# Softmax sums of a cross-attention moved from VectorE to ScalarE, and the work between its units laid out anew

## The chip, the cores and the metric

One core of one Trainium2 chip runs the whole kernel as one program. The metric is the device time of an execution in microseconds, here the median of several runs. The engines are TensorE (PE, matrix products), VectorE (DVE), ScalarE (ACT), GpSimd (POOL) and SyncE (SP, which issues the DMAs); each runs its own list of instructions in order, and semaphores tie the lists together.

## The reference, cut to what matters

The reference is a decoder of two layers on x of 2 x 1024 x 256, all float32, with a layer norm after each part: a quaternion self-attention, a two-hop memory attention on a context of 2 x 77 x 256, eight experts, then in the second layer a long convolution, a cross-attention on the same context, and a quantised gated FFN. The change lies where the convolution part ends and the cross-attention runs:

```python
# convolution part (_L1_attn_ref): K = C * sigmoid(A)**t * B, causal
out = conv(x, K) + D * x
x = _layernorm(x + _layer_norm(x + gelu(out) @ W_proj.T + b_proj, gamma, beta))
# cross-attention (_L1_xattn_ref): 16 heads of 16, keys and values from ctx_1024 (77 rows)
attn = softmax(einsum('bhqd,bhkd->bhqk', q, k) / sqrt(16), axis=-1)
out = einsum('bhqk,bhkd->bhqd', attn, v)
out = out.transpose(0, 2, 1, 3).reshape(B, -1, D) @ Wo.T + bo
x = _layernorm(x + out)
```

## The kernel before, in words

The 2048 rows of x are 16 tiles of 128 rows, in four groups of four. The cross-attention goes through `UX` = 32 units: unit n is tile n // 2 and half n % 2 of the heads (8 heads, `HC`), so a group is 8 units (g = n // 8, m = n % 8). It starts while the last expert and the end of the convolution part (its group 3 of rows, and its norms for groups 2 and 3) are still to be done; these are interleaved with the first 17 units. All orders are written out by hand, one loop over the units for each engine.

A unit goes through these steps. TensorE: `xa_scores(n)` (line 2048) writes the scores of 8 heads x 77 columns into two PSUM banks; two pairs of banks take turns, so scores(n) wait for the exponentials of unit n - 2. VectorE: `lowest(n)` (line 1402) reduces them to one minimum for each head (the scores are computed negated). ScalarE: `numer(n)` (line 777) makes 8 exponentials of 128 x 77 with that minimum as bias. VectorE: `denom(n)` sums them over the 77 columns (line 1409) and takes the reciprocal (line 1410). POOL: `weights(n)` (line 528) multiplies. TensorE: `p_turn(n)` (lines 2062 to 2065) transposes the weights. ScalarE: `p_evac(n)` (lines 787, 788) copies them to SBUF.

In ScalarE's and TensorE's loop, unit n's transposes stand with the scores and exponentials of unit n + 3 (`AHEAD` = 3). TensorE's turn of the loop is scores(n + 3), at m = 4 `queries` of the next group (line 2033), p_turn(n), then what is due there: `xa_values` (lines 2082, 2084) of the group before at m = 0 and 1, `xa_out` (line 2095) at m = 5 and 6, `x_turn4` (line 2026, the next group's rows transposed) at m = 2 (m = 3 for group 0), and at n = 6 `projected(3)` (line 1992), the projection of conv group 3. ScalarE's turn is p_evac(n), copies of transposes (`xT_evac`, line 676), at n = 5 the two gelus of conv group 3 (`conv_gelu`, line 740, another table set, so a table load before and one after), then numer(n + 3). `o_evac` (line 796) copies the values at m = 1 and 2, `q_evac` (line 769) the queries at m = 4. projected(3) waits for both gelus.

VectorE's turn is lowest(n + 3), denom(n + 2), then an entry of the table `between` (line 1457): `convolved(3, k, part)`, part 0 a multiply (line 1309) and a scan (1310), part 1 two more (1314, 1315); `conv_out` (1336), `conv_stats` (1049, 1052), `conv_affine` in two parts of four instructions (1358, 1360), `x_stats` and `x_norm` (1057) for the layer norms, `residual` (1417). POOL's turn is weights(n + 2), then the powers of the norms by the table `XA_LN` (line 74, lines 397 and 399), `x_plus_bproj(3)` at n = 1 (line 515), `x_plus_beta(3)` at n = 5 (line 518) and `x_plus_bo` (line 523) at n = 4, 12 and 20. Behind the 32 units follows the FFN.

Of the kernel before, what the change touches and what calls it, by code (L numbers as in the profile page):

```python
# [13 lines left out]
ALU = mybir.AluOpType  # L14
# [3 lines left out]
P = 128  # L18
# [46 lines left out]
AHEAD = 3  # L65
HP = HC // 2
# [7 lines left out]
XA_LN = {8: (LN_DN[5],), 11: (LN_DN[6],), 14: (LN_DN[7],), 17: (LN_E,), 23: (LN_E + 1,), 30: (LN_E + 2,)}  # L74
# [17 lines left out]
def decoder(nc, a, out):  # L92
    w_kept = nc.dram_tensor("w_kept", (P, 18, D), F32, kind="Internal").ap()
    with ExitStack() as ctx:
# [283 lines left out]
        def _(pool):  # L378
# [175 lines left out]
            for n in range(UX):  # L554
# [4 lines left out]
                if n == 1:  # L559
                    x_plus_bproj(3)  # L560
                if n == 5:
                    x_plus_beta(3)
                for step in XA_LN.get(n, ()):
                    ln_power(step, 4)
                if n % 8 == 4 and n // 8 + 1 < G4:
                    x_plus_bo(n // 8 + 1)
# [16 lines left out]
        def _(act):  # L583
# [187 lines left out]
            def numer(n):  # L771

                act.wait_ge(sem("xa_mn"), n + 1)
                if n >= 4:
                    act.wait_ge(sem("xa_ptr"), n - 3)
                for h in range(HC):
                    ins = act.activation(Ex[n % 4][:, h, :], PS[:, 2 * (n % 2) + h // 4, LC * (h % 4):LC * (h % 4) + LC], ACT.Exp,  # L777
                                         scale=-1.0, bias=mxs[:, 8 * (n % 4) + h:8 * (n % 4) + h + 1])
                ins.then_inc(sem("xa_e"), 1)
# [27 lines left out]
            for n in range(UX):  # L807
# [3 lines left out]
                if m in (1, 2) and g >= 1:  # L811
                    o_evac(g - 1, m - 1)
# [5 lines left out]
                if n == 3:  # L818
                    xT_evac(XA_N[1], 1, 6)
                if n == 5:  # L820
# [5 lines left out]
                if m == 2 and 1 <= g < G4 - 1:  # L826
# [65 lines left out]
        def _(dve):  # L892
# [407 lines left out]
            def convolved(g, k, part):  # L1300
# [4 lines left out]
                if part == 0:  # L1305
                    dve.wait_ge(sem("xgT"), CONV_N[g] + 1)
                    if g or k:
                        dve.wait_ge(sem("conv"), KD * g + k)
                    link(dve.tensor_tensor(conv_z, xt, Apow[:, k, at:at + 4 * P], ALU.mult))
                    link(dve.tensor_tensor_scan(r, ones.to_broadcast([P, 4 * P]), conv_z, carry[:, k:k + 1] if g % 2 else 0.0, ALU.mult, ALU.add))  # L1310
# [37 lines left out]
            def conv_affine(g, part):  # L1348
# [6 lines left out]
                for j in range(4):  # L1355
# [50 lines left out]
            def denom(n):  # L1406
                dve.wait_ge(sem("xa_e"), n + 1)
                sums = mxs[:, 32 + 8 * (n % 4):40 + 8 * (n % 4)]
                link(dve.tensor_reduce(sums, Ex[n % 4], AX.X, ALU.add))
# [47 lines left out]
            between = {2: lambda: (convolved(3, 0, 0), convolved(3, 0, 1)), 3: lambda: convolved(3, 1, 0), 4: lambda: convolved(3, 1, 1),  # L1457
# [789 lines left out]
```

## Time and profile before

| | us |
|---|---|
| median of 3 runs | 787.16 (781.5 to 787.8) |
| the profiled execution | 784.69 |
| its span, first to last instruction | 783.0 |
| TensorE busy in the span | 713.0 (91%) |
| ScalarE busy | 552.9 (71%) |
| VectorE busy | 505.3 (65%) |
| POOL busy | 194.4 (25%) |

The profile is of one execution. Its starts are microseconds from the start of the span. The cross-attention's units lie between about 480 and 617 us. Busy shares are over the whole span, whose stages differ, so they do not say what limits this one. A line such as "x8" merges instructions of one line that follow each other. The granted clock is TensorE's, 1.00 being its full 2.4 GHz.

### The profile page before, as it was taken

The numbers are of one execution on the slowest core, as the hardware profiler recorded it, in microseconds if no ns is written. First come the engines' busy times: TensorE is split into PE (matmuls) and PEld (weight loads), VectorE is DVE, ScalarE is ACT, GpSimd is POOL, SyncE is SP. The second block draws the span as 40 slices with busy tenths as digits, with TensorE's granted clock in tenths as the row PEclk, the third lists the DMA queues.
The fourth block names the chain that finished last, engine by engine and source line by source line (L and its number), as shares of the span: only waits on it lengthen the run. The fifth ranks groups of instructions, "written<-read, shape, count | busy, mean of one in ns | idle before, by whom it ended". The sixth has DMA issues, their size and how long they took to land.

```text
span 783.0 us, 10853 instructions
## 1 busy us (share of the span) xinstructions
PE 713.0 (91%) x3850; PEld 387.3 (49%) x3850; DVE 505.3 (65%) x1181; ACT 552.9 (71%) x977; POOL 194.4 (25%) x246
## 2 busy tenths in 40 slices
PE   4999999989999999999999999889899999992797
PEld 2652222212222225888888886544455644440686
DVE  4794645753413224588647557979877687988776
ACT  3759999999999995464043345587687533898992
POOL 1661142201010000104253242465444100000022
PEclk9999999999999999999999999989899999996799
DMA  7412112141255160303326000010100000000002
GB/s 197 134 32 49 28 28 71 25 95 28 46 142 177 29 182 0 109 2 108 114 101 216 1 1 0 1 70 11 41 1 0 1 1 0 1 0 0 0 28 81
DMA packets 57389, 42.13 MB, mean 54 GB/s; under 512 B 36882, under 2 KB 54136, under 8 KB 57208
## 3 DMA queue, kind: packets, MB, share of 16 engines
q1 hardware_dynamic: 57192, 41.31, 19.1%
q8 instruction: 31, 0.51, 0.3%
q14 instruction: 22, 0.18, 0.1%
q10 hardware_dynamic: 144, 0.13, 0.1%
HBM read 28.59 MB, written 4.46 MB: 42 GB/s over the span
## 4 chain that ended last, share of the span: by engine, by line
PE 56%; ACT 22%; DVE 15%; issue 3%; DMA 1%; SPq 1%; POOL 1%; POOLq 0%; ACTq 0%; DVEq 0%
ACT arena L654 12%; PE banks L1658 8%; PE banks L2207 7%; PE banks L1962 7%; PE banks L1978 6%; PE banks L1644 4%; PE banks L1628 2%; PE banks L1992 2%; ACT arena L878 2%; DVE arena L1486 2%; DVE arena L1049 2%; ACT arena L879 2%; PE banks L1818 2%; ACT arena L867 1%; PE banks L2095 1%
## 5 line engine op out<-in xcount | busy, mean ns | idle before, releaser
L654 ACT ACTIVATE arena<-banks 128x1024 f32<-128x1024 f32 x256 | 239.7, 1047 | 6.5 <-PE banks L1658 4.1
L1658 PE MATMUL banks<-arena 128*32 128x512 f32 x1024 | 136.4, 604 | 2.6 <-DVE arena L1125 2.4
L1644 PE MATMUL banks<-arena 64*128 64x512 f16 x512 | 86.4, 383 | 10.1 <-ACT arena L654 5.8
L2207 PE MATMUL banks<-arena 128*128 128x512 f32 x192 | 83.1, 594 | 1.1 <-DVE arena L1502 0.9
L397 POOL TENSOR_SCALAR arena<-arena 128x2 f32<-128x2 f32 (+2 forms) x39 | 11.8, 302 | 256.2 <-DVE arena L1052 256.2
L1644 PEld LDWEIGHTS banks<-arena 64*128 64x128 f16 x512 | 20.9, 93 | 108.7 <-ACT arena L654 98.9
L777 ACT ACTIVATE arena<-banks,arena 128x77 f32<-128x77 f32 x256 | 59.3, 369 | 19.5 <-DVE arena L1402 19.5
L735 ACT ACTIVATE arena<-banks,arena 128x256 f32<-128x256 f32 x64 | 26.9, 471 | 49.3 <-PE banks L1962 49.3
L2207 PEld LDWEIGHTS banks<-arena 128*128 128x128 f32 x192 | 36.2, 190 | 47.4 <-issue 43.4
L1978 PE MATMUL banks<-arena 128*128 128x256 f32 x256 | 56.5, 380 | 1.2 <-ACT arena L676 1.2
L1962 PE MATMUL banks<-arena 128*128 128x256 f32 x256 | 56.2, 379 | 0.0
L528 POOL TENSOR_TENSOR arena<-arena 128x616 f32<-128x616 f32 x32 | 40.7, 1271 | 56.4 <-DVE arena L1410 56.4
L1978 PEld LDWEIGHTS banks<-arena 128*128 128x128 f32 x256 | 48.2, 190 | 8.6 <-issue 2.2
L1962 PEld LDWEIGHTS banks<-arena 128*128 128x128 f32 x256 | 48.5, 190 | 6.5
L846 ACT ACTIVATE arena<-banks 128x512 f32<-128x512 f32 x48 | 28.1, 609 | 30.4 <-PE banks L2207 30.4
L1057 DVE TENSOR_SCALAR arena<-arena 128x256 f32<-128x256 f32 x96 | 37.4, 442 | 18.1 <-POOL arena L399 18.1
L1125 DVE COPY arena<-banks 128x512 f32<-128x512 f32 x16 | 10.9, 683 | 51.3 <-PE banks L1658 51.3
L2219 PE MATMUL banks<-arena 128*128 128x256 f32 x192 | 41.7, 380 | 0.8 <-ACT arena L886 0.8
L1658 PEld LDWEIGHTS banks<-arena 128*32 128x32 f32 x1024 | 20.4, 107 | 42.7 <-issue 42.7
L1049 DVE BATCH_NORM_STATS2 arena<-arena 128x6 f32<-128x256 f32 x112 | 40.2, 413 | 1.1
L2219 PEld LDWEIGHTS banks<-arena 128*128 128x128 f32 x192 | 36.4, 190 | 6.2 <-ACT arena L886 1.2
L399 POOL TENSOR_TENSOR arena<-arena 128x2 f32<-128x2 f32 (+2 forms) x39 | 36.9, 946 | 3.3
(263 smaller groups left out, 1258.4 us busy)
## 6 DMA issues: line engine op xcount, KB each, us to landing
arena<-in_L_ffn_w SPq DMA_DIRECT2D x16, 1024.0 KB, 7.4
w_kept<-arena SPq DMA_DIRECT2D x3, 768.0 KB, 3.6
arena<-w_kept SPq DMA_DIRECT2D x3, 768.0 KB, 4.7
arena<-in_x SPq DMA_DIRECT2D x4, 512.0 KB, 7.9
out_x<-arena SPq DMA_DIRECT2D x3, 512.0 KB, 2.9
arena<-in_L_ffn_b SPq DMA_DIRECT2D x1, 1024.0 KB, 9.2
arena<-in_L_ffn_w_gate SPq DMA_DIRECT2D x1, 768.0 KB, 7.8
arena<-in_L_ffn_w_up SPq DMA_DIRECT2D x1, 768.0 KB, 9.5
```

The source lines that it names most:

```text
L399: pool.tensor_tensor(rstd[:, at:at + n], veps[:, at:at + n], expo[:, at:at + n], ALU.pow).then_inc(sem("ln_rstd"), 1)
L528: pool.tensor_tensor(Ex[n % 4], Ex[n % 4], rdx[:, n % 4, :, None].to_broadcast([P, HC, LC]), ALU.mult).then_inc(sem("xa_w"), 1)
L654: act.activation(PT[kt % 2][:, half], PS[:, 2 * (n % 3):2 * (n % 3) + 2, :], ACT.Exp, scale=DH ** -0.5 / QK_UP ** 2).then_inc(sem("exp_don ...
L777: ins = act.activation(Ex[n % 4][:, h, :], PS[:, 2 * (n % 2) + h // 4, LC * (h % 4):LC * (h % 4) + LC], ACT.Exp, scale=-1.0, bias=mxs[:, 8 ...
L1049: ins = dve.bn_stats(bstat[:, at + j, :], view(j))
L1057: ins = dve.tensor_scalar(dst(j), src(j), mv[:, at + j, 0:1], rstd[:, at + j:at + j + 1], ALU.subtract, ALU.mult)
L1644: mm = pe.matmul(bank(2 * (n % 3) + h), KT[u % 2][64 * h:64 * h + 64, P * kt:P * kt + P], QT[u % 2][64 * h:64 * h + 64, 512 * half:512 * h ...
L1658: mm = pe.matmul(PS[32 * j:32 * j + 32, 6, :], VS[w][:, kt, h, :], PT[kt % 2][:, half, h, :], start=(kt == 0), stop=(kt == TB - 1))
L1962: mm = pe.matmul(PS[:, f // 2, 256 * (f % 2):256 * (f % 2) + 256], W1r[r][:, k, P * f:P * f + P], XT[:, k, TE * P * e:TE * P * e + TE * P] ...
L1978: mm = pe.matmul(bank(Y_BANK[e])[:, D * j:D * j + D], hT[e % 2][:, f, P * j:P * j + P], W2r[r][:, f, :], start=(f == 0), stop=(f == FT - 1))
L2207: mm = pe.matmul(bank(2 + n % 4), (wgT if n < IC * G4 else wuT)[:, k, P * c:P * c + P], XT[:, k, 512 * g:512 * g + 512], start=(k == 0), s ...
L2219: mm = pe.matmul(o, UF[:, c, P * t:P * t + P], wdT[:, c, :], start=(c == 0), stop=(c == IC - 1))
```

## The change

In units 2 to 17 (`OWN_SUMS`) each of the 8 exponentials writes its own sum (`accum_out`), and `denom` there keeps the reciprocal alone. The sums are of the same values. The entries between the units are laid out anew on all engines: the pieces of conv group 3 are spread over more of VectorE's turns, `conv_gelu(3, k)` goes from ScalarE's turn 5 to 7, `projected(3)` from TensorE's turn 6 to 7, values and their copies of group 0 one turn later, x_turn4(2) one turn later, x_plus_bproj(3), x_plus_beta(3) and x_plus_bo to later turns of POOL.

```diff
--- before.py
+++ after.py
@@ -63,6 +63,8 @@
 
 UX = T * KD
 AHEAD = 3
+OWN_SUMS = range(2, 18)
+VALUES_AT = (1, 0, 0)
 HP = HC // 2
 HEAD2 = P - LC
 SPLIT = LC - HEAD2
@@ -71,7 +73,9 @@
 V_BANK = (7, 6)
 VALUES_IN = {None: (6, slice(0, 512)), 0: (6, slice(0, 256)), 1: (2, slice(256, 512))}
 
-XA_LN = {8: (LN_DN[5],), 11: (LN_DN[6],), 14: (LN_DN[7],), 17: (LN_E,), 23: (LN_E + 1,), 30: (LN_E + 2,)}
+XA_LN = {6: (LN_DN[5],), 9: (LN_DN[6],), 15: (LN_DN[7],), 17: (LN_E,), 23: (LN_E + 1,), 30: (LN_E + 2,)}
+
+XA_BO = (17, 20, 25)
 
 RSQRT_SEED = 0x5F3759DF
 PROJ_BANK = ((6, 7), (6, 7), (5, 7), (6, 7))
@@ -556,14 +560,14 @@
                     weights(n + 2)
                 if n == 0:
                     ln_power(LN_CN[E - 1], 2, 4)
-                if n == 1:
-                    x_plus_bproj(3)
-                if n == 5:
-                    x_plus_beta(3)
                 for step in XA_LN.get(n, ()):
                     ln_power(step, 4)
-                if n % 8 == 4 and n // 8 + 1 < G4:
-                    x_plus_bo(n // 8 + 1)
+                if n == 6:
+                    x_plus_bproj(3)
+                if n == 8:
+                    x_plus_beta(3)
+                if n in XA_BO:
+                    x_plus_bo(1 + XA_BO.index(n))
             for half in range(2):
                 ln_power(LN_E + 3 + half, 2, 2 * half)
             def largest(n, col):
@@ -774,8 +778,10 @@
                 if n >= 4:
                     act.wait_ge(sem("xa_ptr"), n - 3)
                 for h in range(HC):
+                    at = 8 * (n % 4) + h
+                    own = {"accum_out": mxs[:, 32 + at:33 + at]} if n in OWN_SUMS else {}
                     ins = act.activation(Ex[n % 4][:, h, :], PS[:, 2 * (n % 2) + h // 4, LC * (h % 4):LC * (h % 4) + LC], ACT.Exp,
-                                         scale=-1.0, bias=mxs[:, 8 * (n % 4) + h:8 * (n % 4) + h + 1])
+                                         scale=-1.0, bias=mxs[:, at:at + 1], **own)
                 ins.then_inc(sem("xa_e"), 1)
 
             def p_evac(n):
@@ -808,22 +814,22 @@
                 g, m = n // 8, n % 8
                 for i in WQ_AT.get(n, ()):
                     wq_evac(i)
-                if m in (1, 2) and g >= 1:
-                    o_evac(g - 1, m - 1)
+                if g >= 1 and m - VALUES_AT[g - 1] in (1, 2):
+                    o_evac(g - 1, m - VALUES_AT[g - 1] - 1)
                 if m == 4 and g + 1 < G4:
                     q_evac(g + 1)
                 p_evac(n)
                 if n == 2:
                     xT_evac(CONV_N[3], 3, 6)
-                if n == 3:
-                    xT_evac(XA_N[1], 1, 6)
-                if n == 5:
+                if n in (3, 11):
+                    xT_evac(XA_N[g + 1], g + 1, 6)
+                if n == 7:
 
                     conv_gelu(3, 0)
                     conv_gelu(3, 1)
                 if n + AHEAD < UX:
                     numer(n + AHEAD)
-                if m == 2 and 1 <= g < G4 - 1:
+                if m == 2 and g == 2:
                     xT_evac(XA_N[g + 1], g + 1, 6)
                 if n in (UX - 3, UX - 2):
                     o_evac(G4 - 1, n - UX + 3, 0)
@@ -1297,17 +1303,19 @@
                     ins = dve.tensor_scalar(CBrev[:, k, :], Apow[:, k, ::-1], convC[:, k:k + 1], convB[:, k:k + 1], ALU.mult, ALU.mult)
                 link(ins)
 
-            def convolved(g, k, part):
+            def convolved(g, k, part, steps=(0, 1)):
 
                 at = 4 * P * (g % 2)
                 xt = XT[:, k, 4 * P * g:4 * P * g + 4 * P]
                 r = conv_r[g][k]
                 if part == 0:
-                    dve.wait_ge(sem("xgT"), CONV_N[g] + 1)
-                    if g or k:
-                        dve.wait_ge(sem("conv"), KD * g + k)
-                    link(dve.tensor_tensor(conv_z, xt, Apow[:, k, at:at + 4 * P], ALU.mult))
-                    link(dve.tensor_tensor_scan(r, ones.to_broadcast([P, 4 * P]), conv_z, carry[:, k:k + 1] if g % 2 else 0.0, ALU.mult, ALU.add))
+                    if 0 in steps:
+                        dve.wait_ge(sem("xgT"), CONV_N[g] + 1)
+                        if g or k:
+                            dve.wait_ge(sem("conv"), KD * g + k)
+                        link(dve.tensor_tensor(conv_z, xt, Apow[:, k, at:at + 4 * P], ALU.mult))
+                    if 1 in steps:
+                        link(dve.tensor_tensor_scan(r, ones.to_broadcast([P, 4 * P]), conv_z, carry[:, k:k + 1] if g % 2 else 0.0, ALU.mult, ALU.add))
                 else:
                     if g % 2 == 0:
                         dve.tensor_copy(carry[:, k:k + 1], r[:, 4 * P - 1:4 * P])
@@ -1345,14 +1353,14 @@
                 dve.wait_ge(sem("proj_y"), g + 1)
                 stats((lambda j: XB3[g][:, j, :], 4)).then_inc(sem("ln_stat"), 1)
 
-            def conv_affine(g, part):
+            def conv_affine(g, part, tiles=range(4)):
 
                 if part == 0:
                     dve.wait_ge(sem("ln_stat"), LN_DN[2 * g] + 1)
                 else:
                     dve.wait_ge(sem("ln_rstd"), LN_DN[2 * g] + 1)
                     dve.wait_ge(sem("x3_plus"), 2 * g + 2)
-                for j in range(4):
+                for j in tiles:
                     xb = XB3[g][:, j, :]
                     if part == 0:
                         ins = dve.scalar_tensor_tensor(xb, xb, mv[:, j, 0:1], bc1[:, 1, :], ALU.subtract, ALU.mult)
@@ -1406,7 +1414,8 @@
             def denom(n):
                 dve.wait_ge(sem("xa_e"), n + 1)
                 sums = mxs[:, 32 + 8 * (n % 4):40 + 8 * (n % 4)]
-                link(dve.tensor_reduce(sums, Ex[n % 4], AX.X, ALU.add))
+                if n not in OWN_SUMS:
+                    link(dve.tensor_reduce(sums, Ex[n % 4], AX.X, ALU.add))
                 dve.reciprocal(rdx[:, n % 4, :], sums).then_inc(sem("xa_rs"), 1)
 
             def residual(g, half):
@@ -1454,11 +1463,16 @@
             expert_norm(E - 1, 4)
             denom(3)
 
-            between = {2: lambda: (convolved(3, 0, 0), convolved(3, 0, 1)), 3: lambda: convolved(3, 1, 0), 4: lambda: convolved(3, 1, 1),
-                       7: lambda: (conv_out(3), x_stats(2)), 9: lambda: x_norm(LN_DN[5], 2).then_inc(sem("ln_d2"), 1),
-                       10: lambda: conv_stats(3), 11: lambda: conv_affine(3, 0), 12: lambda: conv_affine(3, 1), 13: lambda: x_stats(3),
-                       14: lambda: residual(0, 0), 16: lambda: x_norm(LN_DN[7], 3).then_inc(sem("ln_d2"), 1),
-                       15: lambda: residual(0, 1), 17: lambda: xa_stats(0), 18: lambda: xa_norm(0),
+            between = {2: lambda: convolved(3, 0, 0),
+                       3: lambda: (convolved(3, 0, 1), convolved(3, 1, 0, (0,))),
+                       4: lambda: convolved(3, 1, 0, (1,)), 5: lambda: convolved(3, 1, 1),
+                       6: lambda: x_stats(2), 7: lambda: x_norm(LN_DN[5], 2).then_inc(sem("ln_d2"), 1),
+                       8: lambda: conv_out(3), 9: lambda: conv_stats(3),
+                       10: lambda: conv_affine(3, 0, (0, 1)), 11: lambda: conv_affine(3, 0, (2, 3)),
+                       12: lambda: conv_affine(3, 1, (0, 1)), 13: lambda: conv_affine(3, 1, (2, 3)),
+                       14: lambda: residual(0, 0), 15: lambda: (residual(0, 1), x_stats(3)),
+                       16: lambda: x_norm(LN_DN[7], 3).then_inc(sem("ln_d2"), 1),
+                       17: lambda: xa_stats(0), 18: lambda: xa_norm(0),
                        22: lambda: residual(1, 0), 23: lambda: (residual(1, 1), xa_stats(1)), 24: lambda: xa_norm(1),
                        28: lambda: residual(2, 0), 29: lambda: residual(2, 1), 30: lambda: xa_stats(2), 31: lambda: xa_norm(2)}
             for n in range(2, UX):
@@ -2158,15 +2172,15 @@
                     x_group_turn("ln_c", E, CONV_N[3], 3, b0=6)
                 if g >= 1:
 
-                    if m < KD:
-                        xa_values(g - 1, m, range(NC5))
+                    if 0 <= m - VALUES_AT[g - 1] < KD:
+                        xa_values(g - 1, m - VALUES_AT[g - 1], range(NC5))
 
                     first = 5 if g < G4 - 1 else 3
                     if m in (first, first + 1):
                         xa_out(g - 1, m - first)
-                if m == (2 if g else 3) and g + 1 < G4:
+                if m == (2 if g == 2 else 3) and g + 1 < G4:
                     x_turn4(g + 1)
-                if n == 6:
+                if n == 7:
                     projected(3)
                 if n in (UX - 3, UX - 2):
                     xa_values(G4 - 1, n - UX + 3, range(NC5), 0)
```

## Rows read from the trace of the kernel before

**Rows 1.** Windows of 20 us: length, busy us by engine (instructions), PEclk, DMA.

```profile
490.00:510.00 20.00, 17.95 (x94) 10.73 (x92) 19.10 (x33) 10.79 (x38) 9.09 (x8) 1.00 0.01 1
510.00:530.00 20.00, 16.16 (x75) 9.07 (x75) 15.71 (x28) 17.01 (x57) 11.82 (x7) 0.83 0.22 79
```

**Rows 2.** Waits from 498 to 556 us: total us, times, longest.

```profile
ACT arena L777 <- DVE arena L1402: 11.3, 7, 4.0
...
ACT arena L787 <- PE banks L2065: 1.5, 3, 1.0
```

**Rows 3.** Timeline of ScalarE, memory attention: start us, us, engine line op.

```profile
331.04 0.31 ACT L689 ACTIVATE arena<-banks,arena 128x77 f32<-128x77 f32 x1
331.25 0.20 ACT L689 ACTIVATION_READ_ACCUMULATOR arena<-banks,arena 128x1 f32 x1
331.34 0.32 ACT L689 ACTIVATE arena<-banks,arena 128x77 f32<-128x77 f32 x1
```

**Rows 4.** Timeline of ScalarE, a unit's exponentials and what follows.

```profile
525.92 1.84 ACT L777 ACTIVATE arena<-banks,arena 128x77 f32<-128x77 f32 x8
527.59 0.67 ACT L787 ACTIVATE arena<-banks 128x512 f32<-128x512 f32 x1
```

**Rows 5.** Timeline of VectorE, one unit's denominator.

```profile
529.39 0.78 DVE L1409 TENSOR_REDUCE arena<-arena 128x8 f32<-128x616 f32 x1
530.21 0.20 DVE L1410 RECIPROCAL arena<-arena 128x8 f32<-128x8 f32 x1
```

**Rows 6.** Timeline of POOL and VectorE, conv group 3's two first multiplies.

```profile
501.97 2.35 POOL L515 TENSOR_TENSOR arena<-arena 128x1024 f32<-128x1024 f32 x1
...
502.25 2.62 DVE L1309 TENSOR_TENSOR arena<-arena 128x512 f32<-128x512 f32 x1
...
510.10 0.65 DVE L1309 TENSOR_TENSOR arena<-arena 128x512 f32<-128x512 f32 x1
```

**Rows 7.** Timeline of ScalarE around conv group 3's gelus [idle before].

```profile
509.28 1.84 ACT L777 ACTIVATE arena<-banks,arena 128x77 f32<-128x77 f32 x8 [3.98 <-DVE arena L1402]
...
515.93 0.34 ACT L788 ACTIVATE arena<-banks 128x128 f32<-128x128 f32 x1
516.29 1.28 ACT L740 ACT_TABLE_LOAD   x1
517.58 1.15 ACT L740 ACTIVATE arena<-arena 128x512 f32<-128x512 f32 x2
```

**Rows 8.** Timeline of TensorE, the two slow spells [idle before].

```profile
515.67 1.40 PE L2048 MATMUL banks<-arena 64*128 64x308 f32 x4 [1.28 <-ACT arena L777]
...
518.87 4.58 PE L1992 MATMUL banks<-arena 128*128 128x256 f32 x16
523.39 0.79 PE L2048 MATMUL banks<-arena 64*128 64x308 f32 x4
...
551.90 0.79 PE L2048 MATMUL banks<-arena 64*128 64x308 f32 x4 [0.73 <-ACT arena L777]
...
555.20 1.40 PE L2048 MATMUL banks<-arena 64*128 64x308 f32 x4 [1.46 <-ACT arena L777]
...
558.40 1.94 PE L2082 MATMUL banks<-arena 128*32 128x512 f32 x8
...
561.98 0.79 PE L2048 MATMUL banks<-arena 64*128 64x308 f32 x4
...
563.75 1.06 PE L2082 MATMUL banks<-arena 128*32 128x512 f32 x8
...
565.81 0.79 PE L2048 MATMUL banks<-arena 64*128 64x308 f32 x4
```

**Rows 9.** Windows of 2 us, columns as in rows 1.

```profile
516.00:518.00 2.00, 2.00 (x9) 1.04 (x7) 2.00 (x3) 1.97 (x4) 2.00 (x2) 0.50 0.00 0
556.00:558.00 2.00, 2.00 (x10) 1.09 (x7) 1.97 (x5) 1.53 (x8) 2.00 (x2) 0.50 0.03 8
```

**Rows 10.** Chain that ended last, an earlier group's projection: start us, us.

```profile
481.79 3.65 PE banks L1992 x16
```

## The prediction

> **What bounds the kernel now.** The order of reading was: windows over the stage of the cross-attention (about 480 to 620 us of the span), the waits inside 498 to 556 us, then the timelines of single engines there. The windows show no single bound: from 490 to 510 us VectorE is busy 19.10 of 20 us, TensorE 17.95 and ScalarE only 10.79; in the next 20 us ScalarE is at 17.01 and TensorE's granted clock averages 0.83 [rows 1]. So VectorE is full first, and the cure would seem to be what the change does. But the waits say how much of it can be had. Between 498 and 556 us ScalarE waits 11.3 us for VectorE's minima (line 1402, `lowest`), in 7 waits, and 1.5 us for TensorE's transposes [rows 2]. From 556 us on TensorE runs nearly without a gap until the stage ends, and its time there is the kernel's time. What counts, then, is when TensorE reaches that run.
>
> **The sums on ScalarE.** The trace has this very instruction in another stage: line 689 is an exponential of 128x77 from PSUM with a bias and a sum. Each is followed by a read of the accumulator of 0.20 us, but the pair starts 0.30 us after the pair before it [rows 3]. Without a sum eight take 1.84 us, and the next instruction starts 1.67 us after the first, so 0.21 us each [rows 4]. A unit of eight therefore costs ScalarE 8 x 0.30 = 2.40 instead of 1.67 us, 0.73 more, and its last sum is there 7 x 0.30 + 0.41 = 2.51 us after the first start instead of 1.84, 0.67 more. Over 16 units that is 11.7 us of ScalarE. The ends: nothing, if in a row of eight the reads hid behind the next exponential (the rows with sums stand in groups of at most six); 16 x 8 x 0.20 = 25.6 us, if each read were added whole. I take 11.7, since the pairs' own starts give it.
>
> **The sums off VectorE.** The reduce of line 1409 starts 0.82 us before the reciprocal [rows 5]. Sixteen go, 13.1 us of VectorE in all. On the way of one unit to its weights that is -0.82 + 0.67 = -0.15 us, so nothing: the gain can only be that VectorE comes earlier to the next `lowest`.
>
> **ScalarE's budget.** Of the 16 units, 4 to 17 lie between 498 and 556 us: 14 x 0.73 = 10.2 us more. These waits of ScalarE there are 11.3 + 1.5 = 12.8 us [rows 2]. Even if all of them went, numer(18) could be only 2.6 us earlier. The change takes 13.1 us from a full engine and puts 11.7 on one that has 12.8 us free, in pieces. This is the main term, and it is why I expect little.
>
> **The moved steps.** Before, the scan of conv group 3 was done in one piece behind unit 4's denominator, and its first multiply took 2.62 us beside a POOL addition of 2.35 us, where the next took 0.65 [rows 6]. That piece made numer(6) wait 3.98 us, until 509.28 [rows 7]. After the change POOL's x_plus_bproj(3) is gone from there and only multiply and scan (about 2.8 us) stand in it: lowest(6) can start about 504.7, but ScalarE has then numer(5) with sums and the copy of line 676 to do, so numer(6) starts near 505.8: 3.5 us earlier. The queries of group 1 then begin at 505.8, about as before, and scores(8) follow at 510.5. POOL's x_plus_bproj(3) and x_plus_beta(3) move behind units 6 and 8, where VectorE's x_norm may lose up to 2.4 us beside them; that lies under the stall below. The four affine halves no longer stand whole before a `lowest`. x_plus_bo (POOL, 2.4 us, three times) is needed only by the residuals of units 22, 28 and the end, and moves to 17, 20 and 25: nothing. SP's and POOL's DMA queues are passed by no step; the weights' loads wait for proj_mm, which comes before 530 either way, and are used after 603: nothing.
>
> **A new stall.** Before, the gelu of conv group 3 stood in ScalarE's unit 5 and `projected(3)` in TensorE's unit 6, so one unit lay between them. Now both stand in unit 7. TensorE's order is p_turn(7), projected(3); ScalarE's is p_evac(7), table load, two gelus. The copy cannot start before p_turn(7) ends, so TensorE must idle for 0.7 + 1.28 + 1.15 + 0.1 = 3.2 us (the copy, then load and gelus [rows 7], and the hand-overs). Queued behind it on TensorE are the scores of unit 11, on ScalarE numer(10). ScalarE comes to p_evac(7) only after numer(9), at about 519.8, since each numer before it is 0.73 longer; the gelus end at 522.85 and projected(3) runs from 522.9 to 526.6 at full clock. Before, it ran from 518.87 to 523.39 [rows 8], but had scores(10) and p_turn(7), 1.77 us, still behind it, so that scores(11) came at 525.2. They are 1.4 us later now.
>
> The Trainium skill (ScalarE: Activation LUTs, section What ACT_TABLE_LOAD costs) says that a switch to another table set costs a drain of about 1.38 us beside the load of 1.28. This trace shows the load 0.02 us after the end of the copy and the gelu right behind the load [rows 7], so no such drain there. By the page the stall would be 4.6 instead of 3.2 us, and the forecast 1.4 later.
>
> **From there to unit 17.** After projected(3), ScalarE's unit is 2.40 + 0.65 = 3.05 us and TensorE's 1.8 plus 2.05 for values, 1.0 for a turn, 1.9 for an output product, 3.6 for queries. Worked forward in order, each instruction starting when its engine and its inputs are free: scores(13) start at 532.4, scores(15) at 539.1, queries(2) at 540.25, scores(17) at 549.0, scores(18) at 552.7 and scores(19) at 554.5. Before, the last two were at 551.90 and 555.20 [rows 8]; the second ran at half clock.
>
> **The clock.** The granted clock falls to 0.50 of full (1.2 instead of 2.4 GHz) in two spells, around 516 to 520 and 555 to 561 us [rows 9], each after TensorE had idled. At full clock scores and p_turn take 563.75 - 561.98 = 1.77 us, projected(3)'s sixteen products 3.65 (the same line in an earlier group), values 565.81 - 563.75 = 2.06 [rows 8, 10]. Spell one: 518.87 - 515.67 = 3.20 for scores and turn, 4.52 for projected(3), so 1.43 + 0.87 = 2.3 us lost. Spell two: 3.20 again, and values 561.98 - 558.40 = 3.58, so 1.43 + 1.52 = 3.0 us [rows 8]. The idle before spell two was the 0.73 and 1.46 us ahead of scores(18) and (19) [rows 8]; the working above leaves about 0.3 us of it, so I take the spell as gone: values(1, 0) end at 558.7, where they ended at 561.98, 3.3 us earlier. Spell one stays: TensorE now idles 1.25, 1.15 and 4.2 us between 512 and 523. Some of it falls into the idle itself; I take that 3.7 us of work run at half clock, so 1.8 us lost, of which 0.5 us ScalarE's own pace would have taken anyway: 1.3 us.
>
> **Sum.** -3.3 + 1.3 = -2.0 us. The profiled execution took 784.69 us for a span of 783.0, so 782.7. It lies 2.5 us under the median of the three runs, 787.16 (781.5 to 787.8); against the median the same sum gives 785.2. I write 783.5, nearer the profiled one, since the sum is made on it. Behind 562 us nothing else changes: TensorE is without gaps, x_norm(3) ends near 560.7 as before, x_turn4(3) follows at 564.4, and the shift is carried to the end.
>
> **Rivals.** First, VectorE was the bound all along and the reads cost little: then TensorE's idle of 8.5 us between 498 and 556 and both spells (5.3 us) go, and only the stall of 3.2 stays (8.5 from summing the idle of TensorE's timeline in that stretch, of which rows 8 have the largest still standing, 1.28, 0.73 and 1.46): 784.7 - 8.5 - 5.3 + 3.2 = 774.1. For it: VectorE's 19.10 of 20 us. Against: the budget of ScalarE. Second, half way: sums at their 0.30, but the spell at projected(3) falls wholly into the idle, and the affine's relief is worth more than I give: -6, 778.7. Third, on the other side: TensorE, now waiting for a ScalarE at 3.05 us a unit, idles in pieces of half a microsecond in units 10 to 17, and a third spell of low clock comes on top, while spell two stays. It decides from the point where TensorE's idle in 545 to 556 us is again 2 us. Price: -3.3 becomes -0.3, +1.3 stays, and one spell more is +3.0: +4, 788.7. For it: 2.2 us of idle were enough for spell two. Against: the scores(18) no longer wait for the affine. Fourth, the change doesn't do what it says: the sums are written but the path through ScalarE takes all back, within 1 us of 784.7.
>
> **Chances.** Forecast (-5 to +1 on the profiled time) 0.45; fourth rival 0.20; second 0.13; first 0.08; third 0.14. About 1%, 7.9 us, is what a measurement of this kernel can tell from no change. Faster by over 1%: the first and a third of the second, 0.13; slower by over 1%: 0.05, the third with the upper ends of the reads' cost; within: 0.82. The range 777.5 to 789 leaves out the first rival and the far end of the reads' cost.
>
> **What would show it.** Right: pairs of line 777 at 0.30 us in units 2 to 17, 11 to 12 us more of ScalarE busy, 16 reduces fewer; numer(6) near 505.8; TensorE idle of 3.2 to 4.3 us before line 1992 with a clock of 0.5 near it; no spell near 556. Wrong: reads that add nothing or 0.2 us each; a wait before line 1992 under 2 us; a spell of low clock in units 10 to 17; a gain over 8 us.

## The result, and the profile after

The changed kernel took 790.94 us (median of 12 runs, 789.74 to 793.53) beside 785.64 us for the kernel before (12 runs): ratio 1.0066, 95% interval 1.0049 to 1.0083. It is slower by 5.3 us (5.2 by the ratio) where 2 us less were forecast, and outside the range. Its profiled execution took 791.63 us for a span of 789.9. Four executions of the kernels below (849 us with the gelus in turn 6; 927, 1190 and 1411 us with both edits) were slow ones and count in no ratio.

Section 1 of its page:

```profile
PE 714.6 (90%) x3850; PEld 388.4 (49%) x3850; DVE 494.4 (63%) x1165; ACT 563.9 (71%) x1105; POOL 194.1 (25%) x246
```

The sums went where the change says: VectorE has 16 instructions and 10.9 us less, ScalarE 128 more and 11.0 us more. ScalarE's figure is near the prediction's 11.7. The 16 reduces that went had taken 12.6 us, for 13.1 forecast; VectorE's total fell by less because two norms take 2.0 us longer each, which the shorter steps of conv group 3 make good only in part. The next view is the one of [rows 1], windows of 20 us:

```profile
490.00:510.00 20.00, 17.46 (x97) 11.92 (x96) 17.16 (x39) 15.59 (x81) 9.12 (x9) 1.00 0.00 1
510.00:530.00 20.00, 12.88 (x55) 7.57 (x54) 14.01 (x25) 18.96 (x89) 9.63 (x7) 0.85 0.00 0
...
570.00:590.00 20.00, 17.35 (x80) 10.38 (x79) 14.86 (x26) 13.70 (x51) 11.68 (x10) 0.91 0.04 17
```

VectorE is no longer full (17.16 of 20 us for 19.10), ScalarE is (18.96 between 510 and 530), and TensorE is busy only 12.88 us there, where it was 16.16. A stretch with a lowered clock has appeared at 570 to 590, where the kernel before has none.

The span of this execution is 6.9 us longer than that of before, but not all of it belongs to the change. The projection of conv group 2, ahead of the first changed unit, starts at 485.04 here and at 481.72 before. So starts have to be compared from a common point. I take the start of the sixteen products of the last expert's second tile (491.37 before, 494.69 after) and follow the stage to the first of the transposes behind it that waits (619.27 before, 626.24 after): 127.90 and 131.55 us. The stage costs 3.65 us more. TensorE's waits in it add up to 16.0 us, before to 11.1. TensorE's timeline shows where, as [rows 8] did:

```profile
520.29 0.79 PE L2062 MATMUL banks<-arena 64*128 64x308 f32 x4 [1.26 <-ACT arena L783]
...
526.51 5.83 PE L2006 MATMUL banks<-arena 128*128 128x256 f32 x16 [4.37 <-ACT arena L744]
532.27 0.79 PE L2062 MATMUL banks<-arena 64*128 64x308 f32 x4
...
561.01 0.79 PE L2062 MATMUL banks<-arena 64*128 64x308 f32 x4
...
564.97 0.79 PE L2062 MATMUL banks<-arena 64*128 64x308 f32 x4
...
581.40 0.84 PE L2062 MATMUL banks<-arena 64*128 64x308 f32 x4 [2.65 <-ACT arena L773]
...
584.04 2.66 PE L2109 MATMUL banks<-arena 128*128 128x256 f32 x8
586.63 0.79 PE L2062 MATMUL banks<-arena 64*128 64x308 f32 x4
```

From the common point (the lines of this kernel are numbered some 14 higher): the projection (line 2006 here) starts 4.3 us later than before. Unit 11's scores, at 532.27, are 3.8 us late (37.58 against 525.17 - 491.37 = 33.80). Then the kernel catches up: unit 20's scores at 564.97 are at 70.28, before at 70.61 [rows 8]. The spell of low clock near 556 is gone, as forecast. But unit 24's scores (581.40, before 575.69) are 2.4 us late after a wait of 2.65, and unit 25's (586.63, before 579.66) 3.65 us, because the transposes behind unit 24's scores and the output product at 584.04 ran mostly at low clock. From there nothing changes. So there are two places: one, at 522 to 532, is made good again by 565; the other, at 578 to 586, is not.

The granted clock (last but two of the columns, as in [rows 9]) falls to 0.50, the 1.2 GHz level, at both, each time after TensorE has stood idle:

```profile
524.00:526.00 2.00, 0.00 (x0) 0.00 (x0) 2.00 (x2) 1.97 (x3) 2.00 (x2) 0.50 0.00 0
526.00:528.00 2.00, 1.49 (x4) 1.22 (x5) 1.91 (x4) 1.97 (x4) 1.11 (x1) 0.50 0.00 0
528.00:530.00 2.00, 2.00 (x6) 1.65 (x5) 0.00 (x0) 2.00 (x15) 0.00 (x0) 0.50 0.00 0
...
582.00:584.00 2.00, 2.00 (x9) 1.16 (x7) 1.05 (x2) 1.72 (x8) 2.00 (x2) 0.50 0.00 0
```

What made TensorE wait at 578 is in the timelines of VectorE and POOL. First POOL, then VectorE:

```profile
571.99 2.36 POOL L527 TENSOR_TENSOR arena<-arena 128x1024 f32<-128x1024 f32 x1
```

```profile
572.12 4.25 DVE L1063 TENSOR_SCALAR arena<-arena 128x256 f32<-128x256 f32 x4
576.40 1.22 DVE L1447 TENSOR_REDUCE arena<-arena 128x4 f32<-128x1024 f32 x1
577.53 0.79 DVE L1410 TENSOR_REDUCE arena<-banks 128x8 f32<-128x616 f32 x1
```

```profile
578.36 1.83 ACT L783 ACTIVATE arena<-banks,arena 128x77 f32<-128x77 f32 x8 [3.62 <-DVE arena L1410]
580.03 1.32 ACT L773 ACTIVATE arena<-banks,arena 128x512 f32<-128x512 f32 x2
```

The last two are ScalarE's. Line 527 is x_plus_bo(1), which the change moved from POOL's turn 4 to 17. It begins 0.13 us before VectorE's norm of group 0 (line 1063), whose four instructions took 2.23 us in the kernel before and now take 4.25. Behind the norm on VectorE stands lowest(22), behind that on ScalarE numer(22), which waits 3.62 us, and behind that the copies of the queries of group 3 (line 773), for which unit 24's scores wait.

### The profile page after: what moved, and what is told of

The parts are those of the page before. It is cut to its first block, busy times and chain, and to the rows that moved or that the text cites. A ratio compares the mean times of both kernels' runs of the same rounds, so it can differ in the third digit from the quotient of the medians.

```text
span 789.9 us, 10966 instructions
## 1 busy us (share of the span) xinstructions
PE 714.6 (90%) x3850; PEld 388.4 (49%) x3850; DVE 494.4 (63%) x1165; ACT 563.9 (71%) x1105; POOL 194.1 (25%) x246
## 4 chain that ended last, share of the span: by engine, by line
PE 54%; ACT 29%; DVE 12%; issue 3%; SPq 1%; DMA 1%; POOL 0%; POOLq 0%; ACTq 0%; DVEq 0%
ACT arena L658 14%; PE banks L1672 8%; PE banks L2221 7%; PE banks L1976 7%; PE banks L1992 6%; ACT arena L783 4%; PE banks L1658 4%; PE banks L1642 3%; PE banks L2006 2%; ACT arena L884 2%; DVE arena L1500 2%; ACT arena L885 2%; PE banks L1832 2%; DVE arena L1063 2%; PE banks L2109 2%
## 5 line engine op out<-in xcount | busy, mean ns | idle before, releaser
L783 ACT ACTIVATE arena<-banks,arena 128x77 f32<-128x77 f32 x256 | 70.0, 390 | 11.6 <-DVE arena L1410 11.4
L1063 DVE TENSOR_SCALAR arena<-arena 128x256 f32<-128x256 f32 x96 | 41.4, 483 | 17.4 <-POOL arena L403 17.4
L1131 DVE COPY arena<-banks 128x512 f32<-128x512 f32 x16 | 10.9, 683 | 52.3 <-PE banks L1672 52.3
```

The source lines that it names most:

```text
L1063: ins = dve.tensor_scalar(dst(j), src(j), mv[:, at + j, 0:1], rstd[:, at + j:at + j + 1], ALU.subtract, ALU.mult)
```

## The experiments

The theories at the outset: A, the order of two steps costs the time (the projection that waits for its own turn's gelus; x_plus_bo(1) beside the norm), and the sums cost next to nothing; B, the sums on ScalarE are the cost. "Stage" is the length defined above, from one profile each. "Clock lost" is worked out from windows of 2 us between 486 and 636 us of the same profile, the sum of (1 - granted clock) x 2 us; low clock in which TensorE stood idle is in it, so it is the most that the clock can have cost. Ratios are to the kernel before. The runs in one table, in the order of the text below:

| kernel | ratio (interval) | stage, us | clock lost, us |
|---|---|---|---|
| before | 1 | 127.90 | 6.8 |
| changed | 1.0066 (1.0049 to 1.0083) | 131.55 | 5.1 |
| gelus in turn 6 | 0.9991 (0.9975 to 1.0007) | 126.09 | 0 |
| x_plus_bo in 19 and 21 | 1.0014 (0.9995 to 1.0032) | 128.15 | 3.4 |
| sums alone | 0.9945 (0.9927 to 0.9963) | 124.90 | 1.7 |
| layout alone | 1.0031 (1.0014 to 1.0048) | 130.88 | 5.1 |
| both edits | 0.9949 (0.9923 to 0.9974) | 124.08 | 3.4 |
| both edits, no sums | 0.9969 (0.9947 to 0.9991) | 123.45 | 0 |
| sums, gelus and projection in turn 7 | 1.0001 (0.9981 to 1.0021) | 129.90 | 5.1 |
| sums, x_plus_bo in 17, 20, 25 | 0.9995 (0.9973 to 1.0018) | 127.58 | 3.4 |
| changed, wait filled | 1.0086 (1.0052 to 1.0121) | 134.27 | 3.4 |
| both edits, sums from unit 8 | 0.9954 (0.9931 to 0.9977) | 124.82 | 1.7 |
| sums from unit 8 alone | 0.9971 (0.9949 to 0.9992) | 124.44 | 3.4 |

**Gelus one turn earlier.** In ScalarE's list of the changed kernel:

```diff
-                if n == 7:
+                if n == 6:
                     conv_gelu(3, 0)
                     conv_gelu(3, 1)
```

> The changed kernel with one edit: ScalarE's gelus of conv group 3 stand in its turn 6, TensorE's projection stays in turn 7, so one unit lies between them again. Theory A (the order of two steps costs the time: the projection that waits for its own turn's gelus, and x_plus_bo(1) beside the norm of group 0): TensorE's 4.4 us wait before the projection falls under 1.5 us and the projection runs at full clock in 3.7 instead of 5.8 us; the stage is 4 to 6 us shorter than in the changed kernel, the time at or 1 us under the kernel before. Theory B (the sums on ScalarE are the cost, whatever the order): the wait goes, but ScalarE then holds up each unit, and less than 1.5 us is won.

Measured: 0.9991, against 1.0066 of the changed kernel. For its profile the same kernel was run once more:

> The same kernel as the one with the gelus in turn 6, for its profile: the wait before the projection under 1.5 us, the projection 3.7 us long, and the wait before the scores of unit 24 (2.65 us in the changed kernel) still there.

TensorE's timeline of that run:

```profile
522.60 3.72 PE L2006 MATMUL banks<-arena 128*128 128x256 f32 x16 [1.26 <-ACT arena L744]
526.48 0.79 PE L2062 MATMUL banks<-arena 64*128 64x308 f32 x4 [0.15 <-ACT arena L783]
529.58 0.79 PE L2062 MATMUL banks<-arena 64*128 64x308 f32 x4 [1.26 <-ACT arena L783]
...
576.66 0.79 PE L2062 MATMUL banks<-arena 64*128 64x308 f32 x4 [2.66 <-ACT arena L773]
```

The wait of 4.37 us is 1.26, the projection runs at full clock, the second wait is untouched (2.66). The stage is 5.5 us shorter than in the changed kernel. As A said. But only 3.9 of the 5.5 us are there when unit 24's scores start (82.78 us from the common point, in the changed kernel 86.71). The rest is that no low clock follows the second wait in this profile, as it did in the changed kernel.

**x_plus_bo two turns later.**

```diff
-XA_BO = (17, 20, 25)
+XA_BO = (19, 21, 25)
```

> The changed kernel with one edit: POOL's x_plus_bo of groups 1 and 2 stand in turns 19 and 21 instead of 17 and 20, so that the first no longer runs beside VectorE's norm of group 0. Theory A: the norm's four instructions take 2.2 instead of 4.25 us, TensorE's 2.65 us wait before the scores of unit 24 goes with the low clock after it, 3 to 4.5 us are won against the changed kernel. Theory B: the norm is shorter, but the wait at unit 24 comes from lateness that the sums had made before, so under 1 us is won.

Measured: 1.0014, 0.5% under the changed kernel, about 4 us; the stage is 3.4 us shorter. VectorE and TensorE in this kernel:

```profile
570.66 2.23 DVE L1063 TENSOR_SCALAR arena<-arena 128x256 f32<-128x256 f32 x4
```

```profile
577.93 0.79 PE L2062 MATMUL banks<-arena 64*128 64x308 f32 x4 [0.65 <-ACT arena L773]
578.67 0.63 PE L2076 MATMUL banks<-arena 128*128 128x128 f32 x4
579.14 0.27 PE L2077 MATMUL banks<-arena 128*64 128x128 f32 x1
579.34 0.43 PE L2079 MATMUL banks<-arena 128*64 128x128 f32 x2
579.71 1.99 PE L2109 MATMUL banks<-arena 128*128 128x256 f32 x8
```

The norm is back at 2.23 us, the wait is 0.65 instead of 2.65, the output product 1.99 instead of 2.66. As A said.

**The sums alone.** The kernel before with `OWN_SUMS = range(2, 18)`, `accum_out` in `numer` and the condition in `denom`, nothing moved.

> The kernel before with the sums of units 2 to 17 on ScalarE and nothing moved. Theory A: within 1.5 us of the kernel before, since ScalarE's waits of 11.3 us take the 10.2 us; the low clock near 516 us stays or is a little longer. Theory B: 4 to 6 us slower than the kernel before, as the changed kernel is.

Measured: 0.9945, 782.31 us, so 4.3 us faster by the ratio. Both theories missed: A had the size under 1.5 us, B had the other sign. The stage is 3.0 us shorter. TensorE's timeline, at the two places of [rows 8] and at a third:

```profile
519.90 3.72 PE L1996 MATMUL banks<-arena 128*128 128x256 f32 x16 [1.27 <-ACT arena L741]
...
555.81 0.79 PE L2052 MATMUL banks<-arena 64*128 64x308 f32 x4 [0.43 <-ACT arena L780]
...
593.66 0.79 PE L2052 MATMUL banks<-arena 64*128 64x308 f32 x4 [1.09 <-ACT arena L780]
```

Its waits over the stage add up to what they were before, 11.1 us in both, but none is over 1.3 us. The kernel before had, besides the waits in [rows 8], this longest one ahead of its first spell:

```profile
512.33 0.79 PE L2048 MATMUL banks<-arena 64*128 64x308 f32 x4 [2.37 <-ACT arena L769]
```

Both spells of low clock of the kernel before are gone: the projection takes 3.72 instead of 4.58 us, unit 19's scores 0.79 instead of 1.40. (This profile has one short spell elsewhere, at 594 to 600, after the wait of 1.09 us; the kernel before has that wait and no spell.) So what the sums give here is not less idle but a better clock: 1.7 us lost instead of 6.8. This does not hang on the two profiles alone. The mean granted clock over the whole span was 0.979 to 0.984 in the six runs of this kernel and 0.970 to 0.979 in the 29 of the kernel before; the difference of the means, 0.006 of 785 us, comes to some 5 us, an estimate of the size of the whole gain. It does not say where in the span they lie.

**The layout alone.**

```diff
-OWN_SUMS = range(2, 18)
+OWN_SUMS = range(0)
```

> The changed kernel with all sums on VectorE as before, so the new layout alone. Theory A: as slow as the changed kernel or slower (5 to 7 us over the kernel before), with the wait before the projection at 3.2 us or more and the wait at unit 24 in place. Theory B: faster than the changed kernel by 4 us or more, at the kernel before or under it.

Measured: 1.0031, the stage 3.0 us longer than before. Slower with no sum on ScalarE, so B falls. A had asked for 5 to 7 us and 2.4 came. This is 0.35% less than the changed kernel's 1.0066, with intervals that do not overlap, so in this layout the sums may cost something; but the medians differ by only 1.3 us (789.60 and 790.94, taken beside 787.02 and 785.64 of the kernel before) and the stages by 0.7. How much of the slowdown is the sums' stays open. TensorE:

```profile
524.27 6.24 PE L2006 MATMUL banks<-arena 128*128 128x256 f32 x16 [5.09 <-ACT arena L744]
...
579.14 0.79 PE L2062 MATMUL banks<-arena 64*128 64x308 f32 x4 [2.70 <-ACT arena L773]
```

Both waits are there in full. The wait before the projection does not come from ScalarE being late; it comes from the order.

**Both edits together.**

> The changed kernel with both edits: gelus of conv group 3 in ScalarE's turn 6, x_plus_bo of groups 1 and 2 in turns 19 and 21. Each alone gave back 4 to 5 us of the changed kernel's 5.2. Theory A (two faults of order, which add): both are given back, the time is 2 to 4 us under the kernel before, as with the sums alone (ratio 0.9945). Rival A2 (the lateness that the second fault adds lay behind the first): the two do not add, and the time stays within 1 us of the kernel before.

Measured: 0.9949, the stage 3.8 us shorter than before. The edits gave 0.75 and 0.52% singly and give 1.17% together, so they nearly add, and A2 falls. The ratio rests on seven runs.

**Both edits, no sums on ScalarE.**

> As the kernel with both edits, but all sums on VectorE as before: what the sums are worth in a layout without the two faults. With the sums on ScalarE worth 0.55% in the order of before, theory A expects 3 to 5 us more here than with both edits and the sums on ScalarE; a rival, that the spread pieces of conv group 3 alone do what the sums do, expects the two within 1.5 us.

Measured: 0.9969. The intervals of this and the kernel with the sums overlap, and the stage has the other sign. But the profile is of the fastest of its twelve runs, 779.96 us at a mean granted clock of 0.985: three lie at 780 to 781 us and nine at 784 to 787, at 0.977 to 0.979. A's 3 to 5 us did not come: by the ratios this kernel is 1.6 us slower than the one with the sums, and the intervals allow nothing as well as 3 us. That the spread pieces of conv group 3 do in the new order what the sums do in the old one, as the rival said, fits this and is not shown.

**The first fault by itself.** On the kernel with the sums alone:

```diff
-                if n == 5:
+                if n == 7:
                     conv_gelu(3, 0)
                     conv_gelu(3, 1)
...
-                if n == 6:
+                if n == 7:
                     projected(3)
```

> The kernel before with the sums on ScalarE, and conv group 3's gelus and its projection both moved to turn 7, nothing else: the first fault by itself. Theory A: TensorE waits 3.2 to 4.5 us before the projection and runs it at half clock, and the time is 3 to 5 us over the kernel with the sums alone. Rival: the wait only takes the place of others around it, and under 1.5 us is lost.

Measured: 1.0001 against 0.9945, so 4.4 us. TensorE:

```profile
524.53 6.36 PE L1996 MATMUL banks<-arena 128*128 128x256 f32 x16 [4.37 <-ACT arena L741]
```

The same wait of 4.37 us and the slow projection, in an otherwise old order. As A said. The stage is 5.0 us longer, but 1.7 of that is one more spell, at 506 to 510, which stands ahead of the edit and so is not its own.

**The second fault by itself.** On the kernel with the sums alone, POOL's list:

```diff
-                if n % 8 == 4 and n // 8 + 1 < G4:
-                    x_plus_bo(n // 8 + 1)
+                if n in (17, 20, 25):
+                    x_plus_bo(1 + (17, 20, 25).index(n))
```

> The kernel before with the sums on ScalarE, and POOL's three x_plus_bo in turns 17, 20 and 25 as in the changed kernel, nothing else: the second fault by itself. Theory A: the norm of group 0 takes 4.25 instead of 2.2 us, TensorE waits 2 to 2.7 us before the scores of unit 24, and the time is 2 to 4 us over the kernel with the sums alone (ratio to the kernel before about 0.998 to 1.000). Rival: without the first fault there is slack, and the ratio stays at 0.9945 within 0.001.

Measured: 0.9995 against 0.9945, 3.9 us. TensorE:

```profile
547.84 0.63 PE L2066 MATMUL banks<-arena 128*128 128x128 f32 x4 [0.23 <-ACT arena L791]
576.24 0.79 PE L2052 MATMUL banks<-arena 64*128 64x308 f32 x4 [2.09 <-ACT arena L770]
```

The wait is there, and between these two rows lie 28.4 us, where the kernel with the sums alone has 26.6 (546.88 to 573.49). So the place and the sign are as A said, the profile shows 1.8 us of delay there and a spell behind it (576 to 582). The collision is there too, POOL's addition first and VectorE's norm of group 0 after it:

```profile
566.83 2.35 POOL L524 TENSOR_TENSOR arena<-arena 128x1024 f32<-128x1024 f32 x1
566.95 4.24 DVE L1060 TENSOR_SCALAR arena<-arena 128x256 f32<-128x256 f32 x4
```

Here too a spell ahead of the edit (508 to 512) makes the stages a poor measure.

**The wait filled.** In TensorE's turn 7 of the changed kernel:

```diff
                 if n == 7:
+                    pe.wait_ge(sem("xa_q"), 4)
+                    for _ in range(9):
+                        pe.matmul(bank(6), ident, WpT.rearrange("p k d -> p (k d)"), start=True, stop=True)
                     projected(3)
```

> The changed kernel with nine products of 512 columns of a weight tile into bank 6 just before the projection, 3.9 us of work without use in TensorE's wait of 4.4 us; their result is overwritten. If the idle is what lowers the clock, the wait stays as long but the projection runs in 3.7 instead of 5.8 us, and 1.5 to 2.5 us are won against the changed kernel. Rival: the low clock has another cause (the time since the last spell, or the work of the other engines), and the projection stays at 5 to 6 us with nothing won.

Measured: 1.0086, the stage 2.7 us longer than in the changed kernel. TensorE, then the windows at 523 and 529 us:

```profile
522.35 7.99 PE L2186 MATMUL banks<-arena 128*128 128x512 f32 x18
530.18 3.62 PE L2006 MATMUL banks<-arena 128*128 128x256 f32 x16
533.73 0.79 PE L2062 MATMUL banks<-arena 64*128 64x308 f32 x4
```

```profile
523.00:525.00 2.00, 2.00 (x6) 0.84 (x5) 1.43 (x3) 1.98 (x8) 2.00 (x2) 1.00 0.00 0
...
529.00:531.00 2.00, 2.00 (x8) 1.21 (x7) 0.00 (x0) 1.61 (x11) 0.00 (x0) 1.00 0.00 0
```

The nine products are 18 instructions in the trace, 7.8 us in all, twice what I had reckoned, so they outlasted the wait by 3.5 us and nothing was won; the ratio is higher than the changed kernel's 1.0066, but the intervals overlap. But the clock stayed at full 2.4 GHz at this place, and the projection took 3.62 instead of 5.83 us. ScalarE, VectorE and POOL were busy for the same time over the span as in the changed kernel (563.9, 494.6 and 194.1 us for 563.9, 494.4 and 194.1). The four kernels with a wait of 4.37 us or more at this place all ran the projection at low clock; the one without the idle did not. So the low clock there follows TensorE's idle. Whether a filling of the right length pays was not tried.

**Sums from unit 8 only**, with both edits, and on the kernel before (`OWN_SUMS = range(8, 18)`):

> The kernel with both edits, but sums on ScalarE only in units 8 to 17; units 2 to 7 sum on VectorE. With both edits the sums on ScalarE gave TensorE waits of 1.15, 0.78 and 1.26 us in units 5 to 8, without them it waited 2.51 us for VectorE's conv_out in unit 9. If both are costs of their own, this one has neither and is 1 to 3 us faster than with the sums in 2 to 17, ratio 0.991 to 0.994. Rival: the sums are worth nothing in this layout, and the ratio stays between 0.994 and 0.998.

Measured: 0.9954: no better than with the sums from unit 2, the rival holds. Against the profile with both edits, the wait before unit 7's scores is gone (1.15 us there) and that before unit 9's is 0.56 instead of 1.26, but unit 10's scores wait 1.29 us.

> The kernel before with the sums of units 8 to 17 on ScalarE and nothing moved. If the gain of the sums alone (0.55%) comes from the units where VectorE's affine steps stood before the minima and led to the low clock near 556 us, it is kept whole: ratio 0.993 to 0.996. Rival: it comes from units 2 to 7, where the scan held up unit 6, and then most of it is gone: 0.998 to 1.000.

Measured: 0.9971, between the two expectations. Its profile tells why: the spell near 556 us is gone, the one at the projection is not.

```profile
517.30 0.79 PE L2052 MATMUL banks<-arena 64*128 64x308 f32 x4 [2.38 <-ACT arena L770]
520.65 1.40 PE L2052 MATMUL banks<-arena 64*128 64x308 f32 x4 [1.50 <-ACT arena L780]
523.86 4.78 PE L1996 MATMUL banks<-arena 128*128 128x256 f32 x16
...
559.67 0.79 PE L2052 MATMUL banks<-arena 64*128 64x308 f32 x4 [0.43 <-ACT arena L780]
```

So in these profiles, one of each kernel, the sums of units 8 to 17 take away one spell, those of 2 to 7 the other.

The fastest that I found is the kernel before with the sums alone (0.9945), and level with it the changed kernel with both edits (0.9949); both intervals lie under 1. So do those of three more (0.9954, 0.9969, 0.9971), and all five overlap.

## Why the prediction was wrong

**The sums on ScalarE: price right, worth wrong.** The pairs are 0.30 us apart also in rows of eight, and ScalarE is busy 11.0 us more for 11.7 forecast. ScalarE's waits for VectorE's minima between 498 and 556 us, 11.3 us before, are gone; it still waits 8.0 us there, all for TensorE. (The 12.8 us of the prediction left out a wait of 0.8 us for the queries' products, line 2033.) Two pairs of the changed kernel, then the load and the gelus of conv group 3:

```profile
516.37 0.37 ACT L783 ACTIVATE arena<-banks,arena 128x77 f32<-128x77 f32 x1
516.57 0.25 ACT L783 ACTIVATION_READ_ACCUMULATOR arena<-banks,arena 128x1 f32 x1
516.67 0.38 ACT L783 ACTIVATE arena<-banks,arena 128x77 f32<-128x77 f32 x1
...
524.02 1.28 ACT L744 ACT_TABLE_LOAD   x1
525.31 1.15 ACT L744 ACTIVATE arena<-arena 128x512 f32<-128x512 f32 x2
```

**The new stall: right in place and cause, its clock undersized.** Forecast were a wait of 4.2 us and a start of the projection 4.0 us late; measured 4.37 and 4.3. The kernel without any sums on ScalarE has the wait too (5.09), as the forced order of copy, load, gelus and projection says. The drain beside a table load, which the Trainium skill (ScalarE: Activation LUTs, section What ACT_TABLE_LOAD costs) puts at 1.38 us, is not in this trace either: the gelu starts 1.29 us after the load does. But the spell of low clock ran through nearly the whole projection: 5.76 us from its start to the next instead of 3.65, 2.1 lost where the sum had 1.3.

**The clock spell near 556: right that it goes, its gain oversized.** It went, and values(1, 0) end at 70.28 from the common point instead of 70.61. I had 3.3 - 1.3 = 2.0 us of gain there and 0.3 came: 0.8 of the difference is the spell just named, about as much is units 11 to 19, which took 28.7 us where I had worked out 27.9. The largest wait of this stretch before, the 2.37 us at 512.33, was in the prediction's sum of 8.5 us of idle but not among the waits that it named, nor in its account of spell one. Up to this point the mechanism held and sizes were off.

**The step that failed: "x_plus_bo ... moves to 17, 20 and 25: nothing".** I looked at who needs the addition (the residual of unit 22, far off), and not at what VectorE does in the turn that it was moved to. In the same section I had priced this very collision for x_plus_bproj, from the row of 2.62 us beside POOL's 2.35 [rows 6]; there it came as priced, a norm of 4.30 us at 523.61 under the stall. At x_plus_bo(1) it cost a norm of 4.25 instead of 2.23 us, 2.4 us of delay at unit 24 and 1.3 more by the clock: -0.3 became +3.65. The 1.3 us are of this profile: in the one with the gelus in turn 6 the same wait, 2.66 us, was followed by no low clock. Taking it away gave 3.4 us of the stage and 0.5% of the time; adding it to the kernel with the sums alone cost 3.9 us of the time. The claim "behind 562 us nothing else changes" fell with it.

**The sum.** With this term, 4.0 us, the forecast of -2.0 would have been +2.0, with the two sizes above +3.65. The medians differ by 5.3; the other 1.6 lie ahead of the changed units or in the scatter of the runs, and the profiles don't settle which.

**The rivals.** The third came closest in time (+4), but not in mechanism: the third spell of low clock did come, at unit 24 and not in units 10 to 17, while spell two went. The budget of ScalarE, my main ground for little gain, was sound as a bound on idle time but missed what the sums are worth: the kernel with them alone is 4.3 us faster with TensorE's idle unchanged at 11.1 us, and what differs in the profiles is the clock. That it is the cutting of the waits into short pieces which keeps the clock up is how I read this; no run tests it by itself. In the new layout with both edits no gain of the sums is clear of noise, and the two orders cost more.

## What to carry to other kernels

When a step is moved on one engine, read what every other engine does in the turn it goes to, not only who needs its result: a POOL addition that nobody waits for held up a VectorE norm, and through three engines TensorE. A producer and its consumer put into the same turn on two engines wait for each other once through; one turn between them was worth 0.75% in the changed kernel and 0.56% in the old order. And where TensorE is near the bound, a wait is to be priced with the clock after it: in the changed kernel's profile the waits at the two faults were followed by 2.1 and 1.3 us lost that no wait shows.

## What the runs showed of the hardware that was not expected

The start of the program differs from run to run by more than most effects here. The projection of conv group 2, ahead of all that was edited, starts between 481.4 and 486.7 us in the profiles of these kernels, whose code up to there is the same. In 40 to 70 us of the span the granted clock is 1.00 in the profile of the kernel before and 0.94 in that of the changed kernel, in a stage that neither edits. Whoever compares two profiles by their spans would have put 3.3 us on the change that are not its own.

Which wait lowers the clock was not sharp either. Three waits of 1.26 us, some 3 us apart, left it at full in the kernel with the gelus in turn 6; the kernel with both edits, whose instructions up to there are the same, fell to 0.54 in the window from 516 us on, behind the first of the three (1.26 us, until 515.37):

```profile
516.00:518.00 2.00, 2.00 (x9) 1.13 (x7) 1.97 (x3) 2.00 (x15) 1.19 (x1) 0.54 0.00 0
```

Ahead of 508 us waits of 1.15 and 0.78 us left it at full in the kernel with the sums alone; with x_plus_bo moved as well, which comes later, the same two waits were followed by a spell (508 to 514). And with both edits and no sums on ScalarE, a wait of 2.51 us before the values of unit 9's turn left it at full, as the wait of 2.66 us did with the gelus in turn 6. One spell costs 1.7 to 3.4 us of clock, so a single profile of these kernels can mislead by about the effect in question; the ratios over many runs cannot be read from one.
